# A gated recurrence: the reset gate's input part put into PSUM by ScalarE, and two gates' split products side by side in all 128 steps

## What is computed

```python
def step(h, xs):
    xzt, xrt, xht = xs
    z = jax.nn.sigmoid(xzt + h @ U_z + vz)
    r = jax.nn.sigmoid(xrt + h @ U_r + vr)
    hh = jnp.tanh(xht + r * h @ U + vh)
    h_new = (1.0 - z) * h + z * hh
    return (h_new, h_new)
```

## Time and profile before

| | |
|---|---|
| median of 3 runs | 1515.9 us (1515.52 to 1516.64) |
| span of the profiled execution | 1513.4 us |
| what lies around the span, against the median | 2.5 us |
| PE, PEld | 1503.4 us (99%), 1177.8 us (78%) |
| DVE, ACT, POOL | 1332.9 us (88%), 1066.1 us (70%), 309.1 us (20%) |
| TensorE's granted clock | full speed in all 40 slices |

### The profile page before, as it was taken

The page is one execution under the profiler, slowest core; times in us unless marked ns, Lnnn a source line. Parts: engine busy times, 40 slices in busy tenths (PEclk is TensorE's granted clock), DMA queues, the critical chain, the costliest instruction groups (busy, mean ns, idle before and its releaser), DMA issues.

```text
span 1513.4 us, 58048 instructions
## 1 busy us (share of the span) xinstructions
PE 1503.4 (99%) x24698; PEld 1177.8 (78%) x24698; DVE 1332.9 (88%) x2928; ACT 1066.1 (70%) x2481; POOL 309.1 (20%) x333
## 2 busy tenths in 40 slices
PE   9999999999999999999999999999999999999998
PEld 7874444444444467779999999999999999999998
DVE  7999999999999889888888888888888888877787
ACT  7989999999999833656666666566666666656333
POOL 1100112111110014322222222222222222222222
PEclk9999999999999999999999999999999999999999
DMA  5156465565649978533333333333333333320000
GB/s 198 35 158 189 94 194 139 136 157 145 176 89 143 148 112 82 74 51 23 49 21 49 48 21 49 45 24 49 21 48 47 20 48 30 39 41 4 31 32 31
DMA packets 544979, 116.86 MB, mean 77 GB/s; under 512 B 520144, under 2 KB 527056, under 8 KB 536016
## 3 DMA queue, kind: packets, MB, share of 16 engines
q1 hardware_dynamic: 537424, 82.21, 31.2%
q0 software_dynamic: 7008, 30.41, 10.9%
q10 hardware_dynamic: 288, 0.52, 0.1%
HBM read 66.47 MB, written 33.55 MB: 66 GB/s over the span
## 4 chain that ended last, share of the span: by engine, by line
PE 97%; DVE 2%; issue 1%; ACT 1%; DMA 0%; DVEq 0%
PE ps L1458 33%; PE ps L1560 22%; PE ps L1523 22%; PE ps L1572 12%; PE ps L1544 5%; PE ps L1476 2%; DVE ST L1303 0%; PE ps L1425 0%; DMA AR<-in_w1f 0%; PE ps L1489 0%; DVE RL L1338 0%; DVE AR L1270 0%; DVE HL L1382 0%; DVE ST L1308 0%; DVE ST L1389 0%
## 5 line engine op out<-in xcount | busy, mean ns | idle before, releaser
L1458 PE MATMUL ps<-XH,WH 128*128 128x512 f16 x1872 | 404.7, 379 | 0.0
L1458 PEld LDWEIGHTS ps<-XH,WH 128*128 128x128 f16 x1872 | 182.9, 98 | 220.2 <-issue 0.3
L1560 PE MATMUL ps<-HL,U 128*128 128x64 f16 x8016 | 275.5, 193 | 2.0 <-DVE HL L1382 1.7
L1560 PEld LDWEIGHTS ps<-HL,U 128*128 128x128 f16 x8016 | 259.2, 98 | 8.5 <-issue 3.5
L1675 POOL TENSOR_TENSOR ST<-ST 128x256 f32<-128x256 f32 x127 | 107.9, 849 | 460.5 <-ACT ST L869 460.5
L847 ACT ACTIVATE ST<-ST 128x128 f32<-128x128 f32 x254 | 71.9, 310 | 169.5 <-DVE ST L1303 169.5
L1572 PE MATMUL ps<-HL,U 128*128 128x64 f16 x4064 | 163.2, 194 | 0.0
L1303 DVE SCALAR_TENSOR_TENSOR ST<-ps,dn,AR 128x128 f32<-128x128 f32 (+1 forms) x320 | 108.6, 372 | 46.8 <-PE ps L1572 44.2
L1303 DVE SCALAR_TENSOR_TENSOR ST<-ps,dn,XP 128x128 f32<-128x128 f32 x315 | 107.4, 372 | 41.2 <-PE ps L1572 38.9
L1572 PEld LDWEIGHTS ps<-HL,U 128*128 128x128 f16 x4064 | 138.6, 98 | 0.1
L1560 PEld LDWEIGHTS ps<-RL,U 128*128 128x128 f16 x3952 | 131.9, 98 | 6.0 <-issue 0.9
(11 more groups left out here) (201 smaller groups left out, 2976.4 us busy)
## 6 DMA issues: line engine op xcount, KB each, us to landing
x_scratch<-AR SPq DMA_DIRECT2D x16, 1024.0 KB, 5.3
AR<-in_x POOLq DMA_DIRECT2D x15, 1024.0 KB, 8.1
AR<-HB POOLq DMA_DIRECT2D x11, 1024.0 KB, 7.0
raw<-x_scratch SPq DMA_DIRECT2D x88, 128.0 KB, 4.5
out_y<-raw SPq DMA_DIRECT2D x11, 1024.0 KB, 4.6
raw<-in_x SPq DMA_DIRECT2D x10, 1024.0 KB, 7.4
ST<-in_x SPq DMA_DIRECT2D x5, 1024.0 KB, 7.3
out_y<-AR SPq DMA_DIRECT2D x4, 1024.0 KB, 4.3
```

What stands on the lines that cost most here:

```text
L1458: op = pe.matmul(ps[b][:, :], v[:, g, wp, k, e * P:(e + 1) * P], y[:, xp, k, :], start=n == 0, stop=n == 11)
L1560: pe.matmul(ps[b][:, col:col + B], U[:, g, uh, k, e * P:(e + 1) * P], S[:, k, 0], start=opens, stop=False, skip_group_check=True)
```

## The change

ScalarE writes x's part of the reset gate of step `t + 1` (scaled up to the sums' scale, `uh`) into R's two banks during step `t`, by one ACTIVATE of 128x256 (`put_x`). The matmuls of R add to it from step 2 on (`HELD_FROM`), so DVE's two additions for R are gone, and ScalarE's sigmoid reads the two banks itself. PE's first matmul of R waits for the put in place of DVE's additions. Gates Z and C are side by side in all steps. Nothing else in DVE's, ACT's or PE's order is moved.

```diff
-JOINT = TC
+HELD_FROM = 2
...
         def is_joint(t, g):
 
-            return g != 1 and t < JOINT
+            return g != 1
+
+        def held(t, g):
+
+            return g == 1 and t >= HELD_FROM
...
+            def put_x(t, g):
...
+                banks = PS[:, R[0] * 512:(R[1] + 1) * 512].rearrange("p (h n) -> p h n", h=2)[:, :, 0:2 * B]
+                x = XP[j % 2][:, g].rearrange("p (h e) n -> p h e n", h=2)[:, :, :, tt * B:(tt + 1) * B]
+                act.activation(banks.rearrange("p h (e b) -> p h e b", e=2), x, ACT.Copy, scale=uh[:, g:g + 1]).then_inc(s_put, 1)
...
                     for h in range(2):
-                        act.wait_ge(s_pr, 2 * u + h + 1)
-                        act.activation(two(rg, h), two(rg, h), ACT.Sigmoid).then_inc(s_r, 1)
+                        if held(t, 1):
+                            act.wait_ge(s_R, 2 * u + h + 1)
+                            act.activation(two(rg, h), held_sums(R[h]), ACT.Sigmoid, scale=dn[:, scale(4)]).then_inc(s_r, 1)
+                        else:
+                            act.wait_ge(s_pr, 2 * u + h + 1)
+                            act.activation(two(rg, h), two(rg, h), ACT.Sigmoid).then_inc(s_r, 1)
...
+                    if t + 1 < T and held(t + 1, 1):
+                        put_x(t + 1, 1)
...
-                for h in range(2):
+                for h in range(0 if held(t, 1) else 2):
                     dve.wait_ge(s_R, 2 * u + h + 1)
                     add_x(t, rg, R[h], 1, (2 * h, 2 * h + 1), None, s_pr, 2 * u + h + 1)
...
-                else:
-                    pe.wait_ge(s_pr, 2 * u)
+                elif held(t, 1):
+                    pe.wait_ge(s_put, puts(t, 1))
                 recurrent_first(t, R, 1, HL, s_hhi)
```

More of the change, by code:

```diff
@@ L110, in build @@
         mx, ag, ee, er, up, dn = (sb(n, 15 + NCH) for n in ("mx", "ag", "ee", "er", "up", "dn"))
-        dx1, ux1, bound, dc = sb("dx1", 3), sb("ux1", 3), sb("bound", 4), sb("dc", 3)
+        dx1, ux1, bound, dc, uh = sb("dx1", 3), sb("ux1", 3), sb("bound", 4), sb("dc", 3), sb("uh", 3)
         dx = sb("dx", 3 * NCH)[:, :].rearrange("p (c g) -> p c g", g=3)
@@ L120, in build @@
         hhi, hlo, rhi, rlo = HL[:, :, 0], HL[:, :, 1], RL[:, :, 0], RL[:, :, 1]
-        ps = [ctx.enter_context(nc.psum_tensor(f"ps{i}", [P, 512], F32)) for i in range(8)]
+        PS = ctx.enter_context(nc.psum_tensor("ps", [P, 8 * 512], F32))[:, :]
+        ps = [PS[:, i * 512:(i + 1) * 512] for i in range(8)]
         W1F, W1I, W1H, UZ, UR, UH, CR, CZ, WR, WZ, CH, WH = range(12)
@@ L220, in build @@
         d_last = sem("d_last")
-        s_ones, s_mask, s_lzero = sem("ones"), sem("mask"), sem("lzero")
+        s_mask, s_lzero = sem("mask"), sem("lzero")
         s_hzero = sem("hl_zero")
@@ L246, in build @@
         s_R, s_Z, s_C = sem("R"), sem("Z"), sem("C")
+        s_put = sem("x_in_R")
         s_pr, s_zh, s_pz, s_ch, s_pc = (sem(n) for n in ("prer_", "z_high", "prez_", "c_high", "preh_"))
@@ L387, in is_joint, with puts @@
         def is_joint(t, g):
-            return g != 1 and t < JOINT
+            return g != 1
+        def held(t, g):
+            return g == 1 and t >= HELD_FROM
+        def puts(t, g):
+            return sum(held(n, g) for n in range(t + 1))
         def halved_by_act(t):
@@ L397, in made, with held_sums @@
             return sum(2 if halved_by_act(n) else 1 for n in range(1, t + 1))
+        def held_sums(b):
+            return ps[b][:, 0:2 * B].rearrange("p (e b) -> p e b", e=2)
         def opens_first(t, i):
@@ L731, in put_dv @@
                 put(i, DV[:, turns[i][1]], s_predv)
+            def put_x(t, g):
+                j, tt = divmod(t, TC)
+                if puts(t, g) == 1:
+                    act.wait_ge(s_ux1, 4)
+                if j == 0:
+                    act.wait_ge(s_xpa, KT * (W2_ORDER.index(g) + 1))
+                    act.wait_ge(s_xpb, KT * (B_ORDER.index(g) + 1))
+                else:
+                    act.wait_ge(s_xp, xp_ready(t, g))
+                    if by_seven(j):
+                        act.wait_ge(s_xa, xa_count[turn(j, g, 4)])
+                if t == HELD_FROM:
+                    act.wait_ge(s_pr, 2 * (t - 1))
+                else:
+                    act.wait_ge(s_r, 2 * (t - 1))
+                banks = PS[:, R[0] * 512:(R[1] + 1) * 512].rearrange("p (h n) -> p h n", h=2)[:, :, 0:2 * B]
+                x = XP[j % 2][:, g].rearrange("p (h e) n -> p h e n", h=2)[:, :, :, tt * B:(tt + 1) * B]
+                act.activation(banks.rearrange("p h (e b) -> p h e b", e=2), x, ACT.Copy, scale=uh[:, g:g + 1]).then_inc(s_put, 1)
             def sigmoids(q):
@@ L983, in hidden @@
                 if q == 0:
-                    dve.wait_ge(s_mask, 1)
+                    dve.wait_ge(s_mask, 2)
                 if c not in DIRECT and h == 0:
@@ L1326, in _ @@
                     dve.tensor_tensor(hlo, Hn, hhi, ALU.subtract).then_inc(s_hlo, 1)
+                    for g in range(3):
+                        dve.wait_ge(s_up, scaled(3 + g))
+                        dve.tensor_scalar(uh[:, g:g + 1], up[:, scale(3 + g)], HS, None, ALU.mult).then_inc(s_ux1, 1)
                     evacuate_first(t)
@@ L1555, in recurrent_first @@
                         for k in (2 * kk, 2 * kk + 1):
-                            for uh in ((1,) if joint else (0, 1)):
+                            for half in ((1,) if joint else (0, 1)):
                                 b = banks[e // 2]
                                 col = (e if banks[0] == banks[1] else e % 2) * per
-                                opens = kk == 0 and k == 0 and uh == int(joint) and (e % 2 == 0 if banks[0] != banks[1] else e == 0)
-                                pe.matmul(ps[b][:, col:col + B], U[:, g, uh, k, e * P:(e + 1) * P], S[:, k, 0],
+                                opens = not held(t, g) and kk == 0 and k == 0 and half == int(joint) and (e % 2 == 0 if banks[0] != banks[1] else e == 0)
+                                pe.matmul(ps[b][:, col:col + B], U[:, g, half, k, e * P:(e + 1) * P], S[:, k, 0],
                                           start=opens, stop=False, skip_group_check=True)
@@ L1610, in _ @@
         def _(pool):
-            pool.memset(MK, 1.0).then_inc(s_ones, 1)
-            pool.wait_ge(s_ones, 1)
+            pool.memset(MK, 1.0).then_inc(s_mask, 1)
+            pool.wait_ge(s_mask, 1)
             pool.memset(MK.rearrange("p (s t) -> p s t", t=T)[:, :, 0:1], 0.0).then_inc(s_mask, 1)
```

## The result

The changed kernel takes 1558.8 us (median of 4 runs, 1557.55 to 1558.82), against 1515.7 (4 runs, 1515.13 to 1516.64) for the kernel before: ratio 1.0287, 95% interval 1.0275 to 1.0299. Forecast was 1554 with a range of 1532 to 1580. The span is 1557.0 us, 43.6 more than before, where the sum said 38.1. The time lies 1.8 above the span here (in the kernel before, the median lay 2.5 above it), so the forecast is 5.5 short of the span and 4.8 short of the time.

The account below looks back on a forecast made before the run. PE, busy 99% of the span, was taken to bound the kernel. Losses of 28 us in steps 16 to 103, 1.4, 5.6, 2.8 and 0.6 elsewhere, less 0.3, make +38.1 on 1513.4: span 1551.5, plus 2.5 gives 1554 us, range 1532 to 1580.

Parts of the forecast that it names:

- What bounds the kernel: Whole span: PE, busy 99% and 97% of the chain, sets the time; DVE and ACT count only where PE waits.
- the prize on PE: Z and C side by side take 1.37 each against 1.40: 0.06 less a step, 7 us in 118 steps.
- 81 or 56 ns: PE's matmuls of 128 columns: 56 ns each taken; the rival of 81 ns would give 1650 us, chance 1%.
- The put at nothing: ScalarE's write into R's banks, about 0.4 us after `rhi`, is covered and costs nothing.
- the second rival: DVE's backlog carries over and `rlo` slips too: 0.3 more in 88 steps, 1580 us, chance 10%.
- `rlo`: Between C first and C second: `rlo` starts at 3.89, after Z's pair of 0.91, and PE waits 0.25.
- C's chain: Steps 16 to 103: four additions in two dependent pairs, delayed by DVE's work, start next R late: +0.32 a step, 28 us.
- steps 8 to 15: Longer fill B but the heaviest work before C's additions: 0.7 a step lost, 5.6 us.
- The prediction's first rival: Only `rlo` is late, C's hand-overs being quicker and splits out of the way: 0.17 in 104 steps, 1534 us, chance 12%.
- Steps 112 to 125: No wait for `rlo`, but C's longer chain puts next R at 6.75 against 6.545: 0.2 a step, 2.8 us.
- The last two steps: Steps 126 and 127, at the end of the loop: 0.6 us lost.
- The prize kept: `rlo` isn't late if Z's pair is below 0.66 us: 7 us won, 1508 us, chance 7%.

Follow-up runs that it names:

- Z alone: The changed kernel with C apart from step 8 on, Z side by side in all steps: 1513.8 us, ratio 0.9998.
- C alone: The changed kernel with Z apart from step 8 on, C side by side in all steps: 1524.9 us, ratio 1.0070.
- `rlo` ahead: The changed kernel with DVE's `rlo` moved ahead of Z's two additions in steps 8 to 111: 1547.4 us, ratio 1.0216.
- the last experiment: The changed kernel with Z and C apart again at the end, in steps 112 to 127: 1550.0 us, ratio 1.0232.
- the extra operation: The kernel before with one more dependent 128x256 DVE operation between Z's addition and `rlo` in steps 8 to 111: 1529.1 us, ratio 1.0091.
- small sums: The changed kernel with the four sums of a chunk (L1159) cut to a quarter of their width: 1556.9 us, ratio 1.0278.
- no put: The changed kernel without ScalarE's put, R's additions on DVE as before, Z and C side by side in all steps: 1580.5 us, ratio 1.0434.
- put alone: The kernel before with only ScalarE's put added and R's additions gone, Z and C side by side in steps 1 to 7 alone: 1514.4 us, ratio 0.9998.
- light steps: The kernel before with the extra operation only in the 36 steps from 17 to 111 with neither sum nor split before C's additions: 1515.1 us, ratio 1.0003.
- other steps: The kernel before with the extra operation only in steps 8 to 16 and later ones to 111 with a sum or split: 1528.1 us, ratio 1.0089.

## Why the prediction was right, and where it was off

**What bounds the kernel**, and **the prize on PE**: as said. Z alone shows 1.1 us of it in 88 steps, C alone 0.4; no kernel shows it in its time.

**81 or 56 ns**: 16 matmuls of 128 columns take 0.90 to the next row again (1128.62 to 1129.52), 56 ns each. The Trainium skill's figure of about 81 (TensorE: Matmul & The Clock Gate, section Back-to-back issue gap) is not met here. The rival with 81 ns had 1%.

**The put at nothing**: right; 0.46 us where I estimated 0.4, and the kernel with it alone is level with before. What the step left out is that it is worth 22 us once DVE is waited for. Since the change has both, the sum was not hurt. What the put saves there is a form of the second rival, DVE's backlog, which did come in the kernel without it (`rlo` at 4.49 in step 70).

**`rlo`**: `rlo` at 3.87 (3.89 forecast), wait 0.25 (0.25). The pair is 0.92 to what follows; the first two starts are 0.52 apart. A dependent addition does cost more than a free one, 0.52 from start to start against 0.40 from Z's second addition to `rlo`. The Trainium skill's sentence that a semaphore "costs nothing extra here" (VectorE: DVE Perf Modes, section The DRAIN you can't avoid) is on a row of `tensor_copy` and isn't borne out for these additions; whether the semaphore costs the 0.1 or the reading of what was just written, no run separates.

**C's chain**: forecast additions at 5.22 (sum), 5.01 (light), 5.42 (split) and steps of 7.97, 7.82 and 8.17, mean 7.96. In the chunk from step 72 on, additions are at 5.21, 5.01, 5.40, 5.46, 5.00, 5.22, 5.01, 5.22, and steps last 8.14, 7.88, 8.13, 8.20, 7.76, 7.95, 7.77 and 7.95; over steps 16 to 103 the mean is 700.96 / 88 = 7.965. The 28 us of this term are 28.1, the 1.4 of the next are 1.5. The match to a tenth has some luck in it. Step 16, which the sum costed like those behind it, lasts 9.08 where it was 7.86, 1.2 us by itself, and belongs with steps 8 to 15; the other 87 steps lost 0.31 each and not 0.32. Steps 72 and 91 are 0.2 longer than their like, step 72 because its second pair of additions starts 0.19 later; why was not looked into.

What only the runs show is how the 28 us divide. The prediction's first rival priced a late `rlo` by itself at 0.17 a step; taking it away saves 0.09 on average, since Z's pair then stands ahead of the sum all the same. The whole of it is saved only in steps with neither sum nor split.

**Steps 112 to 125, a term that was too small**: 2.8 forecast, 5.1 measured, 6.91 a step against 6.75. Timeline of the changed kernel, step 117:

```profile
1475.98 1.09 PE L1603 MATMUL ps<-HL,U 128*128 128x64 f16 x32 [0.21 <-DVE HL L1425]
...
1476.47 0.42 DVE L1436 TENSOR_TENSOR HL<-ST,HL 128x256 f16<-128x256 f32 x1
...
1477.04 0.63 PE L1615 MATMUL ps<-HL,U 128*128 128x64 f16 x16
...
1479.83 1.06 PE L1615 MATMUL ps<-RL,U 128*128 128x128 f16 x16
...
1480.51 0.34 DVE L1343 SCALAR_TENSOR_TENSOR ST<-ps,dn,XP 128x128 f32<-128x128 f32 x1
...
1482.90 1.09 PE L1603 MATMUL ps<-HL,U 128*128 128x64 f16 x32 [0.22 <-DVE HL L1425]
```

R second starts 1.06 after R first, where it is 0.93 in the loop. Its weights wait for `hlo` (L1436, done at 1476.89), which in these steps stands behind one more operation of DVE. As long as R came late after `hhi`, as before, that was hidden; now R starts as soon as `hhi` is there, and 0.13 a step is open. I had followed the chain to `hhi` and stopped. Of the other 0.03 a piece is the first addition, 0.68 behind C second and not 0.65. That `hlo` is the cause shows in the other traces: R second starts 0.15 behind the end of `hlo` in every step from 113 to 126 of the changed kernel, of C alone and of `rlo` ahead (0.92 and 1.07 into the step), and of the kernel without the put, where both are later (1.01 and 1.16). In Z alone and in the kernel of the last experiment, with C apart there, `hlo` ends at 0.73 at the latest, and R second starts at 0.93.

**The last two steps**: 0.6 forecast, 3.1 measured. There is no fill any more behind C, so all of C's longer chain is open: step 126 is 1545.39 - 1538.27 = 7.12 where it was 6.02. And the clock fell in step 127, below. Steps 8 to 15, 6.2 for 5.6, were within what I had allowed. So of the 5.5 us that the span is above the sum, 4.8 lie behind step 111, and are these two terms.

**The rivals.** Only `rlo` late (12%) is excluded by `rlo` ahead, which still loses 20 us in 88 steps. A backlog carried over (10%) didn't come: DVE is idle 0.53 before Z's addition in step 72, and in 103 of the 104 steps `rlo` starts at 3.88. The prize kept (7%) had as its point Z's pair below 0.66; it is 0.92. Its idea, that PE's fewer matmuls win by themselves, holds for either gate alone, as far as it goes.

## What to carry to other kernels

Two edits that each cost nothing can use up the same cover: here one makes a product later, the other makes it needed earlier. Cost them together, by the cover that is left, and follow every hand-over that a released engine then meets, the second one (`hlo`) too. The total of a wait in the profile is not what removing it brings; look at what would be waited for next. And an operation that is put beside another engine's can lengthen by half even where neither depends on the other (1.09 to 1.62 here).

## What the runs showed of the hardware that was not expected

**VectorE and GpSimd hold each other up.** A `TENSOR_TENSOR` of 128x512 f32 on VectorE takes 1.09 alone and 1.62 when it starts 0.06 behind GpSimd's product of 0.74; when VectorE is first (1128.48 in step 72, above), it takes its 1.08 and GpSimd's takes 1.40 instead. Both fit the second one standing still until the first is done: 1114.69 + 0.74 = 1115.43, and 1114.75 + 1.62 = 1116.37, 0.94 behind it; 1129.56 for VectorE's end, and 1130.16, 0.60 behind, for GpSimd's. Each time that is 0.14 or 0.15 less than the operation takes alone (GpSimd's takes 0.73). The Trainium skill (SBUF — State Buffer, section SBUF: two separate sides) says so: the one that starts first keeps the shared ports for its whole instruction, and on VectorE's side this concerns, besides some faster modes, operations with two SBUF inputs when GpSimd's reads SBUF, as both do here. The trace agrees. I hadn't used it in the prediction, though the sum of 1.75 stood in the trace of the kernel before; the missed expectation of the extra operation came in part from that.

**TensorE's clock in the last step.** With C side by side in the last steps PE is idle longer ahead of the last gate R, and then runs at half speed. Stretches of the changed kernel's last two steps (us, busy and instructions of PE, PEld, DVE, ACT, POOL, then granted clock, DMA share, GB/s):

```profile
1540.00:1545.30 5.30, 2.70 (x63) 2.53 (x59) 4.64 (x15) 2.21 (x7) 0.76 (x2) 1.00 0.01 5
1545.30:1546.90 1.60, 1.51 (x46) 1.48 (x47) 1.30 (x4) 0.43 (x2) 0.59 (x1) 0.97 0.00 0
1546.90:1549.00 2.10, 2.10 (x34) 2.10 (x31) 1.35 (x4) 0.70 (x2) 0.25 (x1) 0.50 0.47 186
```

and its timeline, where the idle time stands ahead of R (C second follows at 1550.33):

```profile
1545.39 1.09 PE L1603 MATMUL ps<-HL,U 128*128 128x64 f16 x32 [2.69 <-DVE HL L1425]
```

The granted clock is 0.50, 1.2 GHz, from 1546.9 until C second, which starts 4.94 after R, against 1541.63 - 1538.27 = 3.36 one step earlier at full clock (1.00, 2.4 GHz): 1.6 us, most of what the last two steps lost beyond step 126's 1.1. In the kernel with the extra operation in all steps the same fall costs 1.9: C second starts 5.76 after the last R, 3.86 in the kernel before. Of the traces of this study, those of five kernels with an idle time of 2.15 to 2.7 us ahead of the last R (after, C alone, `rlo` ahead, small sums, and no put) all fell to 0.50 in that step. Six with 1.43 to 1.90 kept full clock (before, put alone, Z alone, apart at the end, light steps, other steps), and one with an end like that of before, the kernel with the extra operation in all steps, fell too, after 1.67. So the idle time alone doesn't say when it falls.
